# GpSimd takes the C products of the selective scan in half steps 5 to 26 of the first layer, VectorE writes their B products to PSUM, and attention 0 makes do with two PSUM banks fewer

## Chip, cores and metric

One core of a Trainium2 chip runs the whole program. The metric is the device time in microseconds of one execution. TensorE (PE) multiplies and transposes, VectorE (DVE) does elementwise work, scans and reductions, ScalarE (ACT) does activations and copies, GpSimd (POOL) does elementwise work beside them, and SyncE (SP) issues most of the DMAs.

## The reference, cut to what matters

A two-layer decoder over `x` [4, 256, 256] and a context [4, 256, 128]. Each layer adds an attention branch, a selective state space branch ("xattn") and a feed-forward branch. The change touches the attention and the state space branch of the first layer:

```python
x = x + _L0_attn_ref(_layernorm(x), ...)            # 8 heads of 32, window 64, tanh cap, softmax
x = x + _L0_xattn_ref(ctx, _layernorm(x), ...)

# inside _L0_xattn_ref, for each position of the sequence:
dA = exp(d[..., None] * A)
state = state * dA + (d * u)[..., None] * b[:, None, :]     # 256 channels x 16 states
y = einsum('bdn,bn->bd', state, c)
```

## The kernel before, in words

The 1024 tokens lie on the free axis and the 256 channels in two tiles (`DT` = 2) of 128 partitions. The state space branch is worked off in "half steps" `g`: one of the 16 states for one half (512) of the tokens, so 32 half steps a layer (`LAYER_STEPS`), 0 to 31 in the first layer. Each is one [128, 2, 512] array, 1024 elements per partition, and passes four engines:

- ACT, `ssm_da` (L509): `dA = exp(DEL * A)`, two instructions, each counted in `da_ready`.
- DVE, `ssm_dbu` (L838), the **B product**: `hS = DU * B`, both inputs in SBUF; counted in `dbu_ready`.
- DVE, `ssm_scan` (L846), the **scan**: the recurrence over `dA` and the B product, in place in `hS`; counted in `scan_done`.
- DVE, the **C product** (L849): `hS = hS * C`, in place; counted in `c_ready`.
- PE, `acc` (L1230): eight 128x128 transposes that add the result to PSUM banks 6 and 7; counted in `acc_mm`.

`hS` and `dA` are rings of four half steps, `BCb` holds B and C of four half steps (SP loads one when the C product four half steps back is done, `load_bc`). Every engine has its own instruction stream in the order of the code, and waits on counting semaphores.

Beside the first layer's half steps runs attention 0. Before half step 5, GpSimd does the rotary and norm arithmetic of q, k and v (L375 to L385) between DVE's reductions. Then there are 16 units `u` (`UNITS0`: sequence, group, pair of heads). PE does for each unit the scores `s0(u + 1)` (L1320 to L1322), the transposes back `pv0_tr(u - 1)` (L1346), the product with the values `pv0(u)` (L1334), and then the `acc` of one half step. ACT does the tanh (L575), the exponentials (L581, L582), a copy (L568) and the `ssm_da` of one half step. DVE does `at0(u)` (a reciprocal L944 and a product L947, both read PSUM) after half step `AT0_AT[u]` = 12 + u, so one unit after each of half steps 12 to 27. After unit 8 (`A_TR_UNIT`) the first half of the attention output is transposed (L1354, copied at L954 and L562). Scores used PSUM banks 0 to 3 in two pairs, `pv0` bank 4, `pv0_tr` bank 5. Half steps 28 to 31, the output projection, the gate and the feed-forward branch follow.

In the second layer (half steps 32 to 63) and in the expert stage at the end nothing is changed. The expert stage (L420, L423 on GpSimd, L1203, L1206 on DVE) and one small operation of the routing (L1178) appear in the rows below.

Of the kernel before, what the change touches and what calls it, by code (L numbers as in the profile page):

```python
# [52 lines left out]
STEPS = 2 * 2 * DS  # L53
PAIR_STEPS = DS
# [31 lines left out]
def build(nc, io, out):  # L86
    ctx = ExitStack()
    with ctx:
# [174 lines left out]
        CONV_BANK = [0, 4]  # L263
        ACC_BANK = 6
# [73 lines left out]
        def _(pool):  # L338
# [48 lines left out]
            gp.memset(V0[:, :, D0:D0 + 1], 1.0).then_inc(s["pt0_fill"], 1)  # L387
            ln_rstd(1)
# [64 lines left out]
        def _(act):  # L453
# [101 lines left out]
            for i in range(8):  # L555
                act.wait_ge(s["tr0_mm"], i + 1)
                g, part, hf = i // 4, (i // 2) % 2, i % 2
                dst = (qT0, kT0)[part][:, g, 512 * hf:512 * hf + 512]
                sc.copy(dst, ps[:, 2 + i % 4, :]).then_inc(s["tr0_copied"], 1)
            def a_tr_copy(hf):  # L560
                act.wait_ge(s["a_tr_mm"], 2 * hf + 1)
                sc.copy(aT0[:, 0, 512 * hf:512 * hf + 512], ps[:, 4, :]).then_inc(s["a_tr_act"], 1)  # L562

            def pv0_copy(u):
                act.wait_ge(s["pv0_mm"], u + 1)
                if u:
                    act.wait_ge(s["pv0_tr"], u)
                sc.copy(O0, ps[0:D0 + 1, 4, :]).then_inc(s["pv0_copied"], 1)  # L568

            for u in range(UNITS0):  # L570
# [3 lines left out]
                sb0 = 2 * (u % 2)  # L574
                sc.activation(TH0[u % 2], ps[:, sb0:sb0 + 2, 0:W0 + P], ACT.Tanh, scale=SCORE0).then_inc(s["s0_tanh"], 1)  # L575
# [195 lines left out]
        def _(dve):  # L771
# [56 lines left out]

            def ssm_dbu(g):

                l, pr, n = place(g)
                dve.wait_ge(ld_bc[g % SB_LOADS], 16 * (g // SB_LOADS + 1))
                if g % LAYER_STEPS == 0:
                    dve.wait_ge(s["du_ready"], l + 1)
                if g >= RING:
                    dve.wait_ge(s["acc_mm"], g - RING + 1)
                b = BCb[g % SB_LOADS][:, 0:1, :].broadcast_to([P, DT, HALF])
                v.tensor_tensor(ring(hS, g), DU[:, :, pair(pr)], b, ALU.mult).then_inc(s["dbu_ready"], 1)  # L838

            def ssm_scan(g):  # L840
# [96 lines left out]
            def at0(u):  # L937
# [5 lines left out]
                o = ps[:, 5, 0:4 * (D0 + 1)].rearrange("p (h d) -> p h d", d=D0 + 1)  # L943
# [268 lines left out]
        def _(pe):  # L1212
            mm, tr = nc.tensor.matmul, nc.tensor.transpose

            def conv(l, tiles=range(DT)):

                pe.wait_ge(s["lw_ready"], l + 1)
                pe.wait_ge(ld["ctx"], 16)
                for d in tiles:
# [75 lines left out]
            for i in range(8):  # L1295
# [3 lines left out]
                for t in range(4):  # L1299
# [6 lines left out]
                    last = tr(ps[:, 2 + i % 4, P * t:P * t + P], src, ident[:])  # L1306
# [3 lines left out]
            def s0(u):  # L1310
# [15 lines left out]
            def pv0(u):  # L1326
# [6 lines left out]
                for kb_ in range(2):  # L1333
                    last = mm(ps[0:D0 + 1, 4, :], V0[:, 2 * b + kb_, D0 * g:D0 * g + D0 + 1], PT0[u % 2][:, :, kb_, :],  # L1334
                              start=(kb_ == 0), stop=(kb_ == 1))
                last.then_inc(s["pv0_mm"], 1)

            def pv0_tr(u):
# [4 lines left out]
                for t in range(2):  # L1343
                    for r in range(2):
                        c = (2 * t + r) * (D0 + 1)
                        last = tr(ps[:, 5, c:c + D0 + 1], O0[:, S * r + P * t:S * r + P * t + P], ident[0:D0 + 1, 0:D0 + 1])  # L1346
                last.then_inc(s["pv0_tr"], 1)

            def a_tr(hf):

                pe.wait_ge(s["at0_ready"], UNITS0 if hf else A_TR_UNIT + 1)
                for c in range(HC):
                    for t in range(4):
                        last = tr(ps[:, 4 + c, P * t:P * t + P], H[:, 4 * hf + t, P * c:P * c + P], ident[:])  # L1354
# [486 lines left out]
```

## Time and profile before

| | |
|---|---|
| median of 3 runs | 987.07 us (983.51 to 987.46) |
| the profiled execution | 985.21 us, its span 983.4 us |
| mean granted TensorE clock | 0.912 of full |
| PE busy | 806.8 us (82%) |
| DVE busy | 741.3 us (75%) |
| ACT busy | 459.3 us (47%) |
| POOL busy | 243.4 us (25%) |
| chain that ended last | PE 46%, DVE 30%, issue 11%, ACT 8%, POOL 2% |

Busy shares are over the whole span. The half steps that change start at about 112 us and end at about 230 us of it.

### The profile page before, as it was taken

The numbers are of one execution on the slowest core, as the hardware profiler recorded it, in microseconds if no ns is written. First come the engines' busy times: TensorE is split into PE (matmuls) and PEld (weight loads), VectorE is DVE, ScalarE is ACT, GpSimd is POOL, SyncE is SP. The second block draws the span as 40 slices with busy tenths as digits, with TensorE's granted clock in tenths as the row PEclk, the third lists the DMA queues.
The fourth block names the chain that finished last, engine by engine and source line by source line (L and its number), as shares of the span: only waits on it lengthen the run. The fifth ranks groups of instructions, "written<-read, shape, count | busy, mean of one in ns | idle before, by whom it ended". The sixth has DMA issues, their size and how long they took to land.

```text
span 983.4 us, 11811 instructions
## 1 busy us (share of the span) xinstructions
PE 806.8 (82%) x3952; PEld 577.3 (59%) x3952; DVE 741.3 (75%) x1080; ACT 459.3 (47%) x951; POOL 243.4 (25%) x162
## 2 busy tenths in 40 slices
PE   6822549997788996698998987988984789999997
PEld 3312435555533473466665665656763579999996
DVE  4599899999987897789899788869956744434443
ACT  1422445563114302467666656646773434544542
POOL 1072200000223012101011021111002447666663
PEclk9765658998899999899999999999997799999999
DMA  4222133221502022011111111011200034433431
GB/s 158 91 95 84 44 107 107 107 86 65 203 2 90 22 86 86 3 46 40 63 44 44 44 44 43 23 43 43 88 1 0 1 128 156 149 139 129 157 129 43
DMA packets 24176, 74.60 MB, mean 76 GB/s; under 512 B 3088, under 2 KB 5664, under 8 KB 23744
## 3 DMA queue, kind: packets, MB, share of 16 engines
q1 hardware_dynamic: 23776, 71.51, 20.7%
q10 hardware_dynamic: 352, 2.49, 0.8%
q8 instruction: 25, 0.41, 0.2%
q14 instruction: 23, 0.19, 0.1%
HBM read 72.55 MB, written 1.44 MB: 75 GB/s over the span
## 4 chain that ended last, share of the span: by engine, by line
PE 46%; DVE 30%; issue 11%; ACT 8%; POOL 2%; DMA 0%; POOLq 0%; DVEq 0%; SPq 0%; ACTq 0%
DVE hS L846 10%; PE ps L1457 6%; PE ps L1571 6%; PE ps L1572 6%; PE ps L1573 6%; DVE hS L838 4%; PE ps L1420 4%; PE ps L1536 3%; PE ps L1437 2%; PE ps L1524 2%; PE ps L1222 2%; PE ps L1230 2%; DVE arena L1097 2%; ACT dA L509 1%; PE ps L1515 1%
## 5 line engine op out<-in xcount | busy, mean ns | idle before, releaser
L846 DVE TENSOR_TENSOR_SCAN hS<-dA,hS 128x1024 f32<-128x1024 f32 x64 | 157.8, 2465 | 21.7 <-ACT dA L509 20.5
L1230 PE MATMUL ps<-ident,hS 128*128 128x128 f32 x512 | 75.8, 299 | 49.6 <-DVE hS L849 49.4
L1203 DVE SCALAR_TENSOR_TENSOR arena<-ps,arena 128x1024 f32<-128x1024 f32 x32 | 39.2, 1225 | 102.0 <-ACT arena L724 93.1
L1230 PEld LDWEIGHTS ps<-ident,hS 128*128 128x128 f32 x512 | 64.2, 154 | 77.7 <-DVE hS L849 59.3
L1457 PE MATMUL ps<-WB,hT 128*128 128x512 f32 x192 | 88.7, 606 | 3.8 <-DVE arena L1078 2.0
L509 ACT ACTIVATE dA<-DEL,negA 128x510 f32<-128x510 f32 x128 | 84.8, 717 | 12.3 <-DVE hS L846 11.8
L423 POOL TENSOR_TENSOR MHl<-arena,MHh 128x1024 fp32r<-128x1024 f32 x34 | 81.7, 2404 | 16.7 <-ACT MHh L727 16.7
L849 DVE TENSOR_TENSOR hS<-hS,BCb 128x1024 f32<-128x1024 f32 x64 | 83.6, 1306 | 2.2
L1571 PE MATMUL ps<-Wh,MHh 128*128 128x256 f32 x272 | 77.8, 286 | 6.0 <-POOL MHl L423 6.0
L409 POOL TENSOR_SCALAR jst<-jst 128x8 f32<-128x8 f32 x20 | 12.3, 613 | 279.6 <-DVE jst L1086 279.6
L838 DVE TENSOR_TENSOR hS<-DU,BCb 128x1024 f32<-128x1024 f32 x64 | 77.8, 1216 | 0.1
L1572 PE MATMUL ps<-Wl,MHh 128*128 128x256 f32 x272 | 77.5, 285 | 0.0
L1573 PE MATMUL ps<-Wh,MHl 128*128 128x256 f32 x272 | 77.5, 285 | 0.0
L354 POOL TENSOR_SCALAR lnve<-lnmv 128x4 f32<-128x4 f32 x12 | 4.9, 405 | 268.3 <-DVE lnmv L868 268.2
L1536 PE MATMUL ps<-WA,arena 128*128 128x256 f32 x256 | 65.8, 380 | 2.5 <-DVE X L1135 2.5
L420 POOL TENSOR_TENSOR Wl<-WB,Wh 128x512 fp32r<-128x512 f32 x34 | 47.3, 1393 | 64.2 <-ACT Wh L708 64.2
L1457 PEld LDWEIGHTS ps<-WB,hT 128*128 128x128 f32 x192 | 37.1, 195 | 41.8 <-issue 40.8
L1515 PE MATMUL ps<-ident,arena 128*128 128x128 f32 x192 | 33.5, 285 | 29.4 <-ACT arena L677 24.2
L1571 PEld LDWEIGHTS ps<-Wh,MHh 128*128 128x128 f32 x272 | 52.7, 194 | 8.2 <-POOL MHl L423 7.0
L1571 PE MATMUL ps<-hTh,Wh 128*128 128x512 f32 x136 | 53.8, 396 | 0.0
L1572 PE MATMUL ps<-hTl,Wh 128*128 128x512 f32 x136 | 53.5, 394 | 0.0
L1572 PEld LDWEIGHTS ps<-Wl,MHh 128*128 128x128 f32 x272 | 52.8, 194 | 1.2
(206 smaller groups left out, 1889.5 us busy)
## 6 DMA issues: line engine op xcount, KB each, us to landing
BCb<-bc_dram SPq DMA_DIRECT2D x64, 512.0 KB, 3.6
arena<-gate_dram SPq DMA_DIRECT2D x32, 512.0 KB, 3.7
WB<-in_we SPq DMA_DIRECT2D x34, 256.0 KB, 2.7
WB<-in_wqkv SPq DMA_DIRECT2D x1, 3072.0 KB, 12.9
WA<-in_wo ACTq DMA_DIRECT2D x1, 2048.0 KB, 7.7
WA<-in_ffn SPq DMA_DIRECT2D x1, 1408.0 KB, 6.5
pkb<-in_pk SPq DMA_DIRECT2D x2, 698.0 KB
X<-in_x SPq DMA_DIRECT2D x1, 1024.0 KB, 7.4
```

Source lines behind the costliest of these rows:

```text
L420: gp.tensor_tensor(Wl[:, slot, :], src, Wh[:, slot, :].bitcast(F32), ALU.subtract).then_inc(s["w_lo"], 1)
L423: gp.tensor_tensor(MHl[:, p, :], MH[p], MHh[:, p, :].bitcast(F32), ALU.subtract).then_inc(s["m_lo"], 1)
L509: sc.activation(bands2(ring(dA, g)[:, d, :]), bands2(DEL[:, d, pair(pr)]), ACT.Exp, scale=negA[:, d * DS + n:d * DS + n + 1]).then_inc(s[" ...
L838: v.tensor_tensor(ring(hS, g), DU[:, :, pair(pr)], b, ALU.mult).then_inc(s["dbu_ready"], 1)
L846: v.tensor_tensor_scan(f(h), f(a), f(h), 0.0, ALU.mult, ALU.add).then_inc(s["scan_done"], 1)
L849: v.tensor_tensor(h, h, c, ALU.mult).then_inc(s["c_ready"], 1)
L1230: last = mm(ps[:, ACC_BANK + j // 2, 256 * (j % 2) + P * d:256 * (j % 2) + P * d + P], src[:, d, P * j:P * j + P], ident[:], start=(first ...
L1457: last = mm(ps[:, bank + t, :], hT[:, c, P * (2 * b + t):P * (2 * b + t) + P], WB[:, c, c0:c0 + 512], start=(c == 0), stop=(c == HC - 1))
L1536: last = mm(ps[:, 5, 256 * t:256 * t + 256], aT1[u % 2][:, P * t:P * t + P], WO1[:, h, :], start=(h == 0 and t == 0), stop=(h == H1 - 1), ...
L1571: mm(out, wh, xh, start=start, stop=False, **kw)
L1572: mm(out, wh, xl, start=False, stop=False, **kw)
L1573: return mm(out, wl, xh, start=False, stop=stop, **kw)
```

## The change

A constant `POOL_STEPS = range(5, 27)` names the half steps. For these, DVE writes the B product to PSUM banks 4 and 5 instead of `hS`, waiting for the scan before it, since there is one such buffer; the scan reads it from there and writes `hS`; DVE does no C product; GpSimd does it, in its stream between attention 0's preparation and the next norm. PSUM banks 4 and 5 were attention 0's, which now has one pair of banks for scores (0, 1) and banks 2 and 3 for `pv0` and `pv0_tr`, so `s0(u + 1)` waits for the tanh of unit `u` instead of `u - 1`.

```diff
+POOL_STEPS = range(5, 27)
...
+            def times_c(g):
+
+                pool.wait_ge(s["scan_done"], g + 1)
+                pool.wait_ge(ld_bc[g % SB_LOADS], 16 * (g // SB_LOADS + 1))
+                h = ring(hS, g)
+                gp.tensor_tensor(h, h, BCb[g % SB_LOADS][:, 1:2, :].broadcast_to([P, DT, HALF]), ALU.mult).then_inc(s["c_ready"], 1)
+
+            for g in POOL_STEPS:
+                times_c(g)
             ln_rstd(1)
             ln_rstd(2)
...
-                sb0 = 2 * (u % 2)
-                sc.activation(TH0[u % 2], ps[:, sb0:sb0 + 2, 0:W0 + P], ACT.Tanh, scale=SCORE0).then_inc(s["s0_tanh"], 1)
+                sc.activation(TH0[u % 2], ps[:, 0:2, 0:W0 + P], ACT.Tanh, scale=SCORE0).then_inc(s["s0_tanh"], 1)
...
+            def dbu(g):
+                return ps[:, DBU_BANK:DBU_BANK + 2, :] if g in POOL_STEPS else ring(hS, g)
+
             def ssm_dbu(g):
...
                 b = BCb[g % SB_LOADS][:, 0:1, :].broadcast_to([P, DT, HALF])
-                v.tensor_tensor(ring(hS, g), DU[:, :, pair(pr)], b, ALU.mult).then_inc(s["dbu_ready"], 1)
+                if g in POOL_STEPS:
+                    dve.wait_ge(s["scan_done"], g)
+                    dve.wait_ge(s["qkv0_copied"], NT)
+                v.tensor_tensor(dbu(g), DU[:, :, pair(pr)], b, ALU.mult).then_inc(s["dbu_ready"], 1)
...
-                v.tensor_tensor_scan(f(h), f(a), f(h), 0.0, ALU.mult, ALU.add).then_inc(s["scan_done"], 1)
+                v.tensor_tensor_scan(f(h), f(a), f(dbu(g)), 0.0, ALU.mult, ALU.add).then_inc(s["scan_done"], 1)
+                if g in POOL_STEPS:
+                    return
                 dve.wait_ge(s["scan_done"], g + 1)
+                if g == POOL_STEPS.stop:
+                    dve.wait_ge(s["c_ready"], g)
...
+                if l:
+                    pe.wait_ge(s["scan_done"], POOL_STEPS.stop)
...
-                if u >= 2:
-                    pe.wait_ge(s["s0_tanh"], u - 1)
+                if u:
+                    pe.wait_ge(s["s0_tanh"], u)
                 q0 = S * b
                 for i in range(2):
-                    r, k = 2 * rp + i, 2 * (u % 2) + i
+                    r, k = 2 * rp + i, i
...
-                    last = mm(ps[0:D0 + 1, 4, :], V0[:, 2 * b + kb_, D0 * g:D0 * g + D0 + 1], PT0[u % 2][:, :, kb_, :],
+                    last = mm(ps[0:D0 + 1, 2, :], V0[:, 2 * b + kb_, D0 * g:D0 * g + D0 + 1], PT0[u % 2][:, :, kb_, :],
```

The other lines of the diff only change bank numbers (`tr0` copies, `O0`, `at0`, `a_tr`).

DVE's stream in half steps 13 and 14, each followed by the `at0` of a unit, before (the names in square brackets are the semaphores that an instruction and the wait instructions ahead of it wait for, in their order):

```order
L838 TENSOR_TENSOR hS<-DU,BCb 128x1024 [waits acc_mm,ld_bc1]
L846 SCALAR_TENSOR_TENSOR hS<-dA,hS 128x1024 [waits da_ready,dbu_ready]
L849 TENSOR_TENSOR hS<-hS,BCb 128x1024 [waits scan_done]
L944 RECIPROCAL rden<-ps 128x4 [waits at0_ready,pv0_tr]
L947 TENSOR_TENSOR H<-ps,rden 128x2x64 [waits at0_den]
L838 TENSOR_TENSOR hS<-DU,BCb 128x1024 [waits acc_mm,ld_bc2]
L846 SCALAR_TENSOR_TENSOR hS<-dA,hS 128x1024 [waits da_ready,dbu_ready]
L849 TENSOR_TENSOR hS<-hS,BCb 128x1024 [waits scan_done]
```

and the same place in the changed kernel, where L854 is the B product, L862 the scan, and L964 and L967 are `at0`:

```order
L854 TENSOR_TENSOR ps<-DU,BCb 128x1024 [waits scan_done,qkv0_copied,acc_mm,ld_bc1]
L862 SCALAR_TENSOR_TENSOR hS<-dA,ps 128x1024 [waits da_ready,dbu_ready]
L964 RECIPROCAL rden<-ps 128x4 [waits at0_ready,pv0_tr]
L967 TENSOR_TENSOR H<-ps,rden 128x2x64 [waits at0_den]
L854 TENSOR_TENSOR ps<-DU,BCb 128x1024 [waits scan_done,qkv0_copied,acc_mm,ld_bc2]
L862 SCALAR_TENSOR_TENSOR hS<-dA,ps 128x1024 [waits da_ready,dbu_ready]
```

The C product is gone from DVE's stream, and the B product's list of waits is two longer, with `scan_done` at its head.

GpSimd's stream from the last step of attention 0's preparation on, in the changed kernel; in the kernel before, the first two rows were followed directly by the norm's (L354 there):

```order
L387 TENSOR_TENSOR arena<-arena 128x3072 [waits rope0_rs]
L389 MEMSET arena 128x8 [waits rope0_done]
L395 TENSOR_TENSOR hS<-hS,BCb 128x1024 [waits ld_bc1,scan_done]
L395 TENSOR_TENSOR hS<-hS,BCb 128x1024 [waits ld_bc2,scan_done]
L395 TENSOR_TENSOR hS<-hS,BCb 128x1024 [waits ld_bc3,scan_done]
L395 TENSOR_TENSOR hS<-hS,BCb 128x1024 [waits ld_bc0,scan_done]
```

There are 22 such rows, one for each of half steps 5 to 26, each with `scan_done` as its last wait.

## Rows read from the trace of the kernel before

**Rows 1.** The page: the chain's shares by line, and the costliest groups.
```profile
DVE hS L846 10%; PE ps L1457 6%; PE ps L1571 6%; PE ps L1572 6%; PE ps L1573 6%; DVE hS L838 4%; PE ps L1420 4%; PE ps L1536 3%; PE ps L1437 2%; PE ps L1524 2%; PE ps L1222 2%; PE ps L1230 2%; DVE arena L1097 2%; ACT dA L509 1%; PE ps L1515 1%
...
L423 POOL TENSOR_TENSOR MHl<-arena,MHh 128x1024 fp32r<-128x1024 f32 x34 | 81.7, 2404 | 16.7 <-ACT MHh L727 16.7
...
L420 POOL TENSOR_TENSOR Wl<-WB,Wh 128x512 fp32r<-128x512 f32 x34 | 47.3, 1393 | 64.2 <-ACT Wh L708 64.2
```

**Rows 2.** Table by stretches: us; busy of PE, PEld, DVE, ACT, POOL; clock; DMA.
```profile
127.00:154.00 27.00, 16.59 (x56) 11.13 (x57) 26.59 (x20) 9.94 (x18) 0.00 (x0) 0.51 0.29 101
155.00:195.00 40.00, 39.11 (x210) 23.63 (x210) 38.43 (x39) 23.13 (x42) 0.00 (x0) 1.00 0.28 97
480.00:560.00 80.00, 71.45 (x377) 52.52 (x378) 75.61 (x132) 52.59 (x149) 10.06 (x10) 1.00 0.13 41
```

**Rows 3.** Timeline of DVE (start, us, line), half steps 11 and 12.
```profile
144.44 2.29 DVE L846 TENSOR_TENSOR_SCAN hS<-dA,hS 128x1024 f32<-128x1024 f32 x1
146.76 1.22 DVE L849 TENSOR_TENSOR hS<-hS,BCb 128x1024 f32<-128x1024 f32 x1
...
149.16 2.29 DVE L846 TENSOR_TENSOR_SCAN hS<-dA,hS 128x1024 f32<-128x1024 f32 x1
```

**Rows 4.** Timeline of DVE, half steps 26 and 27.
```profile
224.96 2.29 DVE L846 TENSOR_TENSOR_SCAN hS<-dA,hS 128x1024 f32<-128x1024 f32 x1
...
228.43 0.17 DVE L944 RECIPROCAL rden<-ps 128x4 f32<-128x4 f32 x1
...
228.85 1.22 DVE L838 TENSOR_TENSOR hS<-DU,BCb 128x1024 f32<-128x1024 f32 x1
230.10 2.29 DVE L846 TENSOR_TENSOR_SCAN hS<-dA,hS 128x1024 f32<-128x1024 f32 x1
```

**Rows 5.** Timeline of PE, half steps 17 and 18: first scores of two units.
```profile
180.83 0.30 PE L1320 MATMUL ps<-mask,identb 128*128 128x320 bf16 x1
...
185.91 0.30 PE L1320 MATMUL ps<-mask,identb 128*128 128x320 bf16 x1
```

**Rows 6.** Waits of DVE, 103 to 290 us: total, times, longest.
```profile
DVE hS L846 <- ACT dA L509: 2.5, 1, 2.5
DVE rden L944 <- PE ps L1346: 1.9, 1, 1.9
...
DVE hT L954 <- PE ps L1354: 1.2, 1, 1.2
```

**Rows 7.** Timeline of DVE and POOL, attention 0's preparation at 102 us.
```profile
102.41 0.26 DVE L932 SCALAR_TENSOR_TENSOR arena<-arena 128x96 f32<-128x96 f32 x1
102.58 1.22 DVE L838 TENSOR_TENSOR hS<-DU,BCb 128x1024 f32<-128x1024 f32 x1
102.75 6.28 POOL L385 TENSOR_TENSOR arena<-arena 128x3072 f32<-128x3072 f32 x1 [15.71 <-DVE arena L932]
103.84 7.33 DVE L846 TENSOR_TENSOR_SCAN hS<-dA,hS 128x1024 f32<-128x1024 f32 x1
```

**Rows 8.** Timeline of DVE and POOL, the preparation at 64 us.
```profile
63.94 7.43 POOL L381 TENSOR_TENSOR arena<-arena 128x2560 f32<-128x2560 f32 x1
66.04 6.41 DVE L849 TENSOR_TENSOR hS<-hS,BCb 128x1024 f32<-128x1024 f32 x1
```

**Rows 9.** Timeline of DVE and POOL, the routing at 781 us.
```profile
780.64 2.35 POOL L423 TENSOR_TENSOR MHl<-arena,MHh 128x1024 fp32r<-128x1024 f32 x1 [5.12 <-ACT MHh L727]
780.70 2.35 DVE L1178 TENSOR_SCALAR arena<-arena 128x96 f32<-128x96 f32 x1
```

**Rows 10.** Timeline of DVE and POOL, one expert at 821 us.
```profile
821.55 2.40 POOL L423 TENSOR_TENSOR MHl<-arena,MHh 128x1024 fp32r<-128x1024 f32 x1
...
823.33 1.22 DVE L1203 SCALAR_TENSOR_TENSOR arena<-ps,arena 128x1024 f32<-128x1024 f32 x1 [3.04 <-ACT arena L724]
```

**Rows 11.** Timeline of ACT, then of DVE, at half step 6.
```profile
119.42 1.31 ACT L509 ACTIVATE dA<-DEL,negA 128x510 f32<-128x510 f32 x2
...
120.83 2.29 DVE L846 TENSOR_TENSOR_SCAN hS<-dA,hS 128x1024 f32<-128x1024 f32 x1 [2.54 <-ACT dA L509]
```

More of the change, by code:

```diff
@@ L263, in build @@
         CONV_BANK = [0, 4]
+        DBU_BANK = 4
         ACC_BANK = 6
@@ L558, in _ @@
                 dst = (qT0, kT0)[part][:, g, 512 * hf:512 * hf + 512]
-                sc.copy(dst, ps[:, 2 + i % 4, :]).then_inc(s["tr0_copied"], 1)
+                sc.copy(dst, ps[:, i % 4, :]).then_inc(s["tr0_copied"], 1)
             def a_tr_copy(hf):
                 act.wait_ge(s["a_tr_mm"], 2 * hf + 1)
-                sc.copy(aT0[:, 0, 512 * hf:512 * hf + 512], ps[:, 4, :]).then_inc(s["a_tr_act"], 1)
+                sc.copy(aT0[:, 0, 512 * hf:512 * hf + 512], ps[:, 2, :]).then_inc(s["a_tr_act"], 1)
             def pv0_copy(u):
@@ L567, in pv0_copy @@
                     act.wait_ge(s["pv0_tr"], u)
-                sc.copy(O0, ps[0:D0 + 1, 4, :]).then_inc(s["pv0_copied"], 1)
+                sc.copy(O0, ps[0:D0 + 1, 2, :]).then_inc(s["pv0_copied"], 1)
             for u in range(UNITS0):
@@ L942, in at0 @@
                     dve.wait_ge(s["at0_ready"], u)
-                o = ps[:, 5, 0:4 * (D0 + 1)].rearrange("p (h d) -> p h d", d=D0 + 1)
+                o = ps[:, 3, 0:4 * (D0 + 1)].rearrange("p (h d) -> p h d", d=D0 + 1)
                 v.reciprocal(rden0[:], o[:, :, D0 * (1 - g)]).then_inc(s["at0_den"], 1)
@@ L953, in a_tr_copy @@
                 dve.wait_ge(s["a_tr_mm"], 2 * hf + 2)
-                v.tensor_copy(aT0[:, 1, 512 * hf:512 * hf + 512], ps[:, 5, :]).then_inc(s["a_tr_dve"], 1)
+                v.tensor_copy(aT0[:, 1, 512 * hf:512 * hf + 512], ps[:, 3, :]).then_inc(s["a_tr_dve"], 1)
             for g in range(4, LAYER_STEPS - 4):
@@ L1305, in _ @@
                         src = K40[:, 4 * hf + t, g, :]
-                    last = tr(ps[:, 2 + i % 4, P * t:P * t + P], src, ident[:])
+                    last = tr(ps[:, i % 4, P * t:P * t + P], src, ident[:])
                 last.then_inc(s["tr0_mm"], 1)
@@ L1345, in pv0_tr @@
                         c = (2 * t + r) * (D0 + 1)
-                        last = tr(ps[:, 5, c:c + D0 + 1], O0[:, S * r + P * t:S * r + P * t + P], ident[0:D0 + 1, 0:D0 + 1])
+                        last = tr(ps[:, 3, c:c + D0 + 1], O0[:, S * r + P * t:S * r + P * t + P], ident[0:D0 + 1, 0:D0 + 1])
                 last.then_inc(s["pv0_tr"], 1)
@@ L1353, in a_tr @@
                     for t in range(4):
-                        last = tr(ps[:, 4 + c, P * t:P * t + P], H[:, 4 * hf + t, P * c:P * c + P], ident[:])
+                        last = tr(ps[:, 2 + c, P * t:P * t + P], H[:, 4 * hf + t, P * c:P * c + P], ident[:])
                     last.then_inc(s["a_tr_mm"], 1)
```

## Prediction

> **What bounds the kernel now.** I read the page first, for which lines hold the chain that ended last; then the table by stretches, for which engine is full where the change works; then DVE's timeline through one half step of each kind; then what DVE waited for; and last the places where GpSimd and DVE work at the same time, because the change makes them do so 22 times.
>
> DVE's scan is the line with the largest share of the chain (10%), its B product has 4% [rows 1]. Between 127 and 154 us DVE is busy for 26.59 of 27 us and PE for 16.59, at a granted clock of 0.51, its lower level of 1.2 GHz. Between 155 and 195 us, with attention units beside the half steps, both are full: DVE 38.43 and PE 39.11 of 40 us, PE now at 2.4 GHz [rows 2]. A half step without a unit takes DVE 4.72 us from scan to scan (144.44 to 149.16): scan 2.29, C product 1.22, B product 1.22, with small overlaps [rows 3]. With a unit it takes 5.14 us (224.96 to 230.10); from the unit's reciprocal to the next B product are 0.42 us [rows 4]. PE's period there is 5.08 us (180.83 to 185.91) [rows 5]. So DVE sets the pace up to half step 12, and after it DVE and PE set it together. DVE's idle time in this part is small: 2.5 us before the scan of half step 6, for ACT, and 1.9 and 1.2 us around the transposes after unit 8, for PE [rows 6].
>
> The stretch that I compare runs from the scan of half step 6 at 120.83 us [rows 11] to that of half step 27 at 230.10 us [rows 4]: **109.27 us for 21 half steps**.
>
> **The change part by part.** *Removed from DVE:* 22 C products of 1.22 us. If nothing took their place, a half step would go from 4.72 to about 3.6 us, and from 5.14 to about 4.0.
>
> *Added on GpSimd:* 22 products of 128x1024. The nearest row is the same operation on as many elements in the expert stage, 2.404 us over 34 of them [rows 1]. In themselves they would fit beside a scan of 2.29 us plus a B product.
>
> *Whether the two run side by side* is what decides. The trace says when they do not. At 103.84 us a scan with both inputs in SBUF starts 1.09 us into a GpSimd product and takes 7.33 us in place of 2.29; it ends at 111.17, 2.14 us after GpSimd's end at 109.03 [rows 7]. At 66.04 us a C product takes 6.41 us and ends at 72.45, 1.08 us after GpSimd's end at 71.37 [rows 8]. So a DVE instruction with two SBUF inputs stands until GpSimd's ends. The order is by who starts first: the B product at 102.58 us, 0.17 us ahead of GpSimd, keeps its 1.22 us [rows 7]; a small DVE operation at 780.70 us, 0.06 us behind GpSimd's start, is held for GpSimd's whole 2.35 us [rows 9]. A lead of 0.06 us is enough.
>
> The scan is taken out of this: it now has one SBUF input and one in PSUM, and such an instruction of the expert stage keeps 1.22 us while GpSimd works beside it (823.33 against an end at 823.95) [rows 10]. That row also says that reading PSUM costs nothing over SBUF. But the B product still reads DU and B from SBUF, and the C product and the next B product are both released by the same `scan_done`.
>
> *Who starts first after a scan.* GpSimd: its instruction waits on `scan_done` itself, and in rows 7 it starts 0.08 us after the DVE instruction that it waits for (102.67 to 102.75). DVE: in half steps 12 to 26 it does the unit's two operations first, 0.42 us. In half steps 6 to 11 the B product comes directly, but with four semaphores, `scan_done` at the head of the list and two others between it and the instruction. What a wait ahead of an instruction takes is seen at half step 6: ACT's end at 120.73, scan at 120.83, 0.10 us with one such wait [rows 11]; with more behind it I take about 0.2 us. So **GpSimd starts first every time**, and DVE's next B product stands until the C product ends.
>
> *The half step then is* 0.08 (GpSimd's start after the scan) + 2.40 (C product) + 1.08 (what remains of the B product after GpSimd's end, rows 8) + 0.03 (B product to scan, 103.80 to 103.84 in rows 7) + 2.29 (scan) = **5.88 us**, with a unit or without, since the unit's 0.42 us lie beside the C product. The scan and the C product never overlap, so writing the B product to PSUM gains nothing.
>
> *The sum.* 21 x 5.88 = 123.5 us, less 109.27, is **+14.2 us**. The first C product (half step 5) costs nothing: it and the B product behind it end at about 119.4 us, and the scan of half step 6 waits for ACT until 120.83 in any case. The 3.1 us of idle time around unit 8 are inside the 109.27; in the changed kernel DVE waits for PE while the C product runs anyway. After half step 27 DVE's stream is as before and has little idle time, so the delay reaches the end.
>
> *The price of the C product.* The trace does not show this very operation. Lower bound: the 2560-element product of rows 8, which itself stood until the scan before it ended (about 66.01), then took 5.36 us, 2.09 ns per element, 2.14 us for 1024. Upper bound: twice the 512-element product, 2 x 1.39 = 2.79 us [rows 1]. I take 2.40, the same shape. The ends give 5.62 and 6.27 us per half step, +8.7 and +22.4 us. The Trainium skill (GPSIMD Engine Reference, section 3.1, Elementwise) has 4497 ns for an elementwise operation of two inputs over 2048 elements; halved, as an estimate, that is 2.25 us, and the sum would be +11.1 us.
>
> *Small parts, together.* DVE writing to PSUM is in no row; reading is free by rows 10, I bound it by 0.05 us per half step to either side, 1 us in all, and take nothing. The single pair of score banks: in steady state a tanh follows its scores at once and PE comes to the next scores only after a `pv0` and an `acc`, so the wait is over by then; only at the first unit does PE stand for about 0.8 us, with half steps of work in hand. The ring of four: a C product ends about 2.5 us after its scan instead of 1.2, while `acc_mm` and the B and C loads are asked for three half steps later. PE's new `scan_done` wait in `conv` is met before PE comes to it.
>
> **The rivals.**
> *A, DVE is first in half steps 6 to 11* (its waits cost less than GpSimd's 0.08 us). Then a B product of 1.22, a C product beside the scan, and 3.57 us per half step: 6 x 3.57 + 15 x 5.88 = 109.6, +0.3 us, 987.4. Rows 3 speak for it (0.03 us from a scan to the instruction that waits on it alone); the list of waits speaks against it.
> *B, faster: the two run side by side throughout* (a product into PSUM is not held, or DVE gets its B product in first even behind the unit). DVE needs 3.57 and 4.0 us, and PE becomes the bound at 5.08 us per unit: 6 x 1.15 + 15 x 0.06 = 7.8 us saved, 979.3. It decides if the C products end after the following B product has run at its plain 1.22 us. Rows 7 to 9 speak against it. By the Trainium skill (SBUF — State Buffer, section "Who interferes with whom") two SBUF inputs on DVE stand against a GpSimd operation that reads SBUF, whichever starts first holding the shared ports throughout; by that rule rival B needs DVE to start first behind the units too, and the trace agrees with the rule in rows 7 to 10.
> *C, slower still: PE falls back to the lower clock.* It would be busy for 5.08 of 5.88 us, 86%. Where five units of fifteen fall to 1.2 GHz, each needs PE for about 10.2 us in place of 5.88; two of the five are taken up by half steps that PE is ahead, and three cost 4.3 us each, 13 us, 1014. Against it: 71.45 of 80 us busy (89%) kept the clock at 1.00 [rows 2].
>
> **How the numbers follow.** The forecast has 0.74, A 0.10, B 0.10, C 0.06. The profiled execution took 985.21 us; the same +14.2 on the median of 987.07 gives **1001.3 us**. The range reaches down to A's end at 987 and up to 1009 (the upper bound of the C product, 22.4 us, is the end itself). About 0.5%, 5 us, is what a measurement of this kernel can tell from no change. Faster: B, 0.10. Same: A, 0.10. Slower: the forecast and C, 0.80.
>
> **What would show it.** Right: GpSimd's C products start about 0.08 us after each scan; B products in half steps 6 to 27 show some 3 us in place of 1.22 (about 3.3 without a unit before them, 3.1 with one); scans stay at 2.29; scans are 5.88 us apart. Wrong: B products at 1.22 us and C products of 3.5 us or more (DVE first: rival A or B), scans above 2.3 us (PSUM as a scan input is dear, or it is held too), or C products well off 2.40.

## The result, and the profile of the changed kernel

| | before | changed |
|---|---|---|
| median of 4 runs of each, us | 985.29 (982.5 to 987.46) | 1003.56 (1002.07 to 1005.95) |
| ratio of the times, 95% interval | | 1.0194 (1.0157 to 1.0232) |
| profiled execution, us (its span) | 985.21 (983.4) | 1002.07 (1000.3) |
| scan of half step 6 to scan of half step 27, us | 109.27 | 124.84 |

The change makes the kernel 1.9% slower. In the profiled executions the span is 16.9 us longer, and the stretch in which the C products moved is 15.6 us longer. The forecast was 1001.3 us and +14.2 us.

The page of the changed kernel, with the span, the busy times and the shares of the chain that ended last (it answers to [rows 1]):

```profile
span 1000.3 us, 11858 instructions
PE 808.5 (81%) x3952; PEld 578.7 (58%) x3952; DVE 753.5 (75%) x1058; ACT 459.3 (46%) x951; POOL 293.7 (29%) x184
DVE hS L862 7%; PE ps L1479 6%; PE ps L1593 6%; DVE ps L854 5%; PE ps L1594 5%; PE ps L1595 5%; PE ps L1442 4%; PE ps L1558 3%; PE ps L1459 2%; DVE hS L854 2%; PE ps L1252 2%; PE ps L1546 2%; PE ps L1244 2%; DVE arena L1117 2%; ACT dA L520 2%
```

L862 is the scan now and L854 the B product. The B product that writes to PSUM ("ps") stands in the chain with 5% of its own, beside 2% for the half steps that still write it to SBUF ("hS"). The scan's share fell from 10% to 7%. A hold by GpSimd shows as nothing but a larger share of the B product; L395 isn't among the lines of the chain, since no semaphore marks the end of the hold.

The same instructions by line, all half steps (duration in ns, least, median and longest; then first and last start, and the shape; L395 is GpSimd's C product):

```profile
L854 DVE TENSOR_TENSOR hS<-DU,BCb x42: 1191/1218/3198, 51.7 to 732.9; 128x1024 f32<-128x1024 f32 x42
L854 DVE TENSOR_TENSOR ps<-DU,BCb x22: 1224/3208/3317, 110.6 to 234.7; 128x1024 f32<-128x1024 f32 x22
L862 DVE TENSOR_TENSOR_SCAN hS<-dA,ps x22: 2286/2287/2287, 111.9 to 237.9; 128x1024 f32<-128x1024 f32 x22
L395 POOL TENSOR_TENSOR hS<-hS,BCb x22: 2341/2352/2368, 114.3 to 240.3; 128x1024 f32<-128x1024 f32 x22
```

These four rows are nearly the whole story. The same B product has a median of 1.22 us in the half steps where GpSimd does no C product and 3.21 us where it does. Of the 22 B products that come behind a C product of GpSimd's, 18 take 3.19 to 3.32 us. The other four, of half steps 21 to 24, come later because DVE waited for PE at unit 8: two run after GpSimd's end at 1.22 us, two catch its last part and take 1.99 and 2.75 us. The scan stays at 2.29 us in all 22 half steps. GpSimd's product is even, 2.34 to 2.37 us, so it is never the one that is held.

DVE and GpSimd through one half step without a unit (11 to 12) and one with a unit (18 to 19); start, duration, line, and in brackets the idle time before with what ended it:

```profile
148.10 2.29 DVE L862 TENSOR_TENSOR_SCAN hS<-dA,ps 128x1024 f32<-128x1024 f32 x1
150.47 2.34 POOL L395 TENSOR_TENSOR hS<-hS,BCb 128x1024 f32<-128x1024 f32 x1 [3.49 <-DVE hS L862]
150.59 3.31 DVE L854 TENSOR_TENSOR ps<-DU,BCb 128x1024 f32<-128x1024 f32 x1 [0.20 <-DVE hS L862]
153.93 2.29 DVE L862 TENSOR_TENSOR_SCAN hS<-dA,ps 128x1024 f32<-128x1024 f32 x1
...
188.99 2.29 DVE L862 TENSOR_TENSOR_SCAN hS<-dA,ps 128x1024 f32<-128x1024 f32 x1
191.19 0.16 DVE L964 RECIPROCAL rden<-ps 128x4 f32<-128x4 f32 x1
191.35 2.36 POOL L395 TENSOR_TENSOR hS<-hS,BCb 128x1024 f32<-128x1024 f32 x1 [3.49 <-DVE hS L862]
191.38 0.29 DVE L967 TENSOR_TENSOR H<-ps,rden 128x128 f32<-128x128 f32 x1
191.59 3.21 DVE L854 TENSOR_TENSOR ps<-DU,BCb 128x1024 f32<-128x1024 f32 x1
194.83 2.29 DVE L862 TENSOR_TENSOR_SCAN hS<-dA,ps 128x1024 f32<-128x1024 f32 x1
```

The scan ends at 150.39. GpSimd starts 0.08 us later, DVE 0.20 us later, and the B product then ends at 153.90, 1.09 us after GpSimd's end at 152.81. From scan to scan that is 5.83 us without a unit and 5.84 with one, where [rows 3] and [rows 4] had 4.72 and 5.14. GpSimd's idle time of 3.49 us before each product shows that it had time to spare: it is not the bound, only in the way.

What DVE waited for between 103 and 300 us (total, times, longest; [rows 6] before):

```profile
DVE rden L964 <- PE ps L1368: 4.7, 3, 3.3
DVE hT L974 <- PE ps L1376: 2.1, 1, 2.1
...
DVE ps L854 <- DVE hS L862: 1.4, 7, 0.2
DVE hS L862 <- ACT dA L520: 1.2, 1, 1.2
```

The third row shown is the 0.20 us by which DVE comes late, seven times (half steps 5 to 11). Rows one and two are waits for PE around the transposes after unit 8. A held B product isn't in this view at all: the hold is booked as duration.

The changed kernel by stretches (busy time of PE, PEld, DVE, ACT, POOL, then the granted clock of PE, DMA share, GB/s), the first two to set beside [rows 2]:

```profile
127.00:154.00 27.00, 12.00 (x48) 8.93 (x49) 25.82 (x11) 8.74 (x15) 11.74 (x5) 0.57 0.23 79
160.00:198.00 38.00, 36.89 (x195) 21.77 (x194) 37.55 (x28) 23.09 (x41) 14.91 (x7) 1.00 0.29 96
199.00:209.00 10.00, 4.77 (x12) 2.11 (x12) 7.83 (x7) 3.24 (x6) 2.89 (x2) 0.50 0.34 107
428.00:448.00 20.00, 16.94 (x85) 12.99 (x84) 16.06 (x28) 13.69 (x40) 2.10 (x3) 0.91 0.07 27
608.00:638.00 30.00, 25.87 (x119) 17.61 (x118) 25.91 (x48) 16.56 (x50) 2.74 (x2) 0.94 0.11 36
```

DVE still reads as full (37.55 of 38 us), but some 2 us of each half step are an instruction that stands. PE holds 2.4 GHz beside the units and is at 1.2 GHz around unit 8 (0.50). What PE did before that, in the changed kernel and then in the kernel before (the first transposes after unit 8):

```profile
203.40 1.97 PE L1376 MATMUL ps<-ident,H 128*128 128x128 f32 x8 [5.33 <-DVE H L967]
```

```profile
194.27 1.09 PE L1354 MATMUL ps<-ident,H 128*128 128x128 f32 x8 [0.89 <-DVE H L947]
```

The transposes need DVE's result of unit 8. DVE now takes 5.84 us for a half step of which PE's part takes 5.08. PE, behind at first (15.00 busy of 15 us from 160 to 175 and again from 175 to 190), waits for DVE for the first time at 191 us, and at unit 8 it stands for 5.33 us in place of 0.89. The granted clock is 0.50 from 199 to 203 us, where PE does nothing, and the same eight transposes then take 1.97 us in place of 1.09.

**Where the 16.9 us are.** The scan of half step 6 starts at 118.91 us, 1.9 us earlier than before. Of this 1.7 us are there already at the scan of half step 4 (102.11 us against 103.84), where nothing is changed yet; over the thirteen traces of this case that scan starts between 100.6 and 104.1 us. The stretch adds 15.6. From the scan of half step 27 to the end 3.2 us more pass (756.6 against 753.3 us). Two steps of about 1.2 and 1.7 us make most of the last term; they lie in the second layer's attention, between 428 and 448 and between 608 and 638 us, where the granted clock was 0.91 and 0.94 in this execution and 1.00 in the execution before, over the same work. They don't belong to the change: the changed kernel with earlier units (the last experiment below) takes 751.5 us from the same scan to the end, and two executions of one other kernel, B product first with units earlier, take 760.2 and 755.1 us.

### The profile page after: what moved, and what is told of

The parts are those of the page before. It is cut to its first block, busy times and chain, and to the rows that moved or that the text cites. A ratio compares the mean times of both kernels' runs of the same rounds, so it can differ in the third digit from the quotient of the medians.

```text
span 1000.3 us, 11858 instructions
## 1 busy us (share of the span) xinstructions
PE 808.5 (81%) x3952; PEld 578.7 (58%) x3952; DVE 753.5 (75%) x1058; ACT 459.3 (46%) x951; POOL 293.7 (29%) x184
## 4 chain that ended last, share of the span: by engine, by line
PE 47%; DVE 29%; issue 11%; ACT 8%; POOL 2%; DMA 1%; DVEq 0%; POOLq 0%; SPq 0%; ACTq 0%
DVE hS L862 7%; PE ps L1479 6%; PE ps L1593 6%; DVE ps L854 5%; PE ps L1594 5%; PE ps L1595 5%; PE ps L1442 4%; PE ps L1558 3%; PE ps L1459 2%; DVE hS L854 2%; PE ps L1252 2%; PE ps L1546 2%; PE ps L1244 2%; DVE arena L1117 2%; ACT dA L520 2%
## 5 line engine op out<-in xcount | busy, mean ns | idle before, releaser
L862 DVE TENSOR_TENSOR_SCAN hS<-dA,hS 128x1024 f32<-128x1024 f32 x42 | 105.9, 2522 | 18.4 <-ACT dA L520 17.9
L434 POOL TENSOR_TENSOR MHl<-arena,MHh 128x1024 fp32r<-128x1024 f32 x34 | 81.8, 2405 | 16.9 <-ACT MHh L737 16.9
L395 POOL TENSOR_TENSOR hS<-hS,BCb 128x1024 f32<-128x1024 f32 x22 | 51.8, 2352 | 83.4 <-DVE hS L862 83.4
L854 DVE TENSOR_TENSOR ps<-DU,BCb 128x1024 f32<-128x1024 f32 x22 | 63.7, 2894 | 1.4 <-DVE hS L862 1.4
L869 DVE TENSOR_TENSOR hS<-hS,BCb 128x1024 f32<-128x1024 f32 x42 | 56.6, 1348 | 1.4
L854 DVE TENSOR_TENSOR hS<-DU,BCb 128x1024 f32<-128x1024 f32 x42 | 54.1, 1289 | 0.1
```

Source lines behind the costliest of these rows:

```text
L395: gp.tensor_tensor(h, h, BCb[g % SB_LOADS][:, 1:2, :].broadcast_to([P, DT, HALF]), ALU.mult).then_inc(s["c_ready"], 1)
L434: gp.tensor_tensor(MHl[:, p, :], MH[p], MHh[:, p, :].bitcast(F32), ALU.subtract).then_inc(s["m_lo"], 1)
L854: v.tensor_tensor(dbu(g), DU[:, :, pair(pr)], b, ALU.mult).then_inc(s["dbu_ready"], 1)
L862: v.tensor_tensor_scan(f(h), f(a), f(dbu(g)), 0.0, ALU.mult, ALU.add).then_inc(s["scan_done"], 1)
L869: v.tensor_tensor(h, h, c, ALU.mult).then_inc(s["c_ready"], 1)
```

## The experiments

The forecast rests on three claims: (1) a two-SBUF-input instruction of DVE stands while GpSimd's runs, and all of the loss is that; (2) who starts first after a scan decides, by hundredths of a microsecond; (3) the new waits, the PSUM destination and the single pair of score banks cost nothing. The eleven runs, of ten kernels, take these apart. All compute the whole reference. Line numbers shift by one or two where an edit adds lines. Each ratio is against the kernel before, run on the same chip.

### First four: who is first, and what the rest costs

**B product first.** In GpSimd's `times_c`, one wait more:

```
             def times_c(g):
+                pool.wait_ge(s["dbu_ready"], g + 2)
                 pool.wait_ge(s["scan_done"], g + 1)
```

GpSimd's C product of half step g now waits until DVE's B product of half step g + 1 has ended.

> GpSimd's C product g waits, beside the scan g, for the B product g + 1; all else as in the changed kernel. Theory (the one that starts first holds the other off, and in the changed kernel GpSimd is first): every B product is back at 1.22 us, the C product starts 0.1 us after it and runs 2.35 us beside the scan, which has one input in PSUM and stays at 2.29. Half steps 6 to 11 take 3.6 to 3.75 us in place of 5.84, those with a unit are set by PE at 5.08 us: some 14 us less than the changed kernel from there alone and 11 us from the rest, a time of about 978 to 980 us, 5 to 8 us under the kernel before. Rival (two engines' operations on SBUF hold each other off whatever the inputs are): the scan is held until the C product ends, half steps of 1.2 + 2.4 + 2.2 = 5.8 us, about 1003 us as the changed kernel.

Measured: 981.85 us against 984.42, ratio 0.9982 (0.9947 to 1.0016); the stretch takes 106.55 us. DVE and GpSimd over two half steps:

```profile
123.39 1.23 DVE L855 TENSOR_TENSOR ps<-DU,BCb 128x1024 f32<-128x1024 f32 x1 [0.20 <-DVE hS L863]
124.66 2.29 DVE L863 TENSOR_TENSOR_SCAN hS<-dA,ps 128x1024 f32<-128x1024 f32 x1
124.70 2.36 POOL L396 TENSOR_TENSOR hS<-hS,BCb 128x1024 f32<-128x1024 f32 x1 [4.82 <-DVE ps L855]
127.15 1.23 DVE L855 TENSOR_TENSOR ps<-DU,BCb 128x1024 f32<-128x1024 f32 x1 [0.20 <-DVE hS L863]
128.42 2.29 DVE L863 TENSOR_TENSOR_SCAN hS<-dA,ps 128x1024 f32<-128x1024 f32 x1
```

Scan (2.29) and C product (2.36) run side by side at their own prices, the B product is back at 1.23, and a half step without a unit takes 3.76 us. A single line of waiting turns 1.9% slower into no measurable difference. But it is less than was expected (978 to 980 us). DVE's waits of this kernel from 103 to 300 us, one of the instructions behind the first of them, the last C product on GpSimd with what stands around it, and three stretches of the table:

```profile
DVE rden L965 <- PE ps L1369: 22.2, 14, 4.1
...
DVE hS L870 <- POOL hS L396: 2.3, 1, 2.3
```

```profile
148.06 0.18 DVE L965 RECIPROCAL rden<-ps 128x4 f32<-128x4 f32 x1 [2.33 <-PE ps L1369]
...
227.46 2.29 DVE L863 TENSOR_TENSOR_SCAN hS<-dA,hS 128x1024 f32<-128x1024 f32 x1
227.50 4.40 POOL L396 TENSOR_TENSOR hS<-hS,BCb 128x1024 f32<-128x1024 f32 x1 [1.50 <-DVE hS L855]
...
232.01 1.23 DVE L870 TENSOR_TENSOR hS<-hS,BCb 128x1024 f32<-128x1024 f32 x1 [2.26 <-POOL hS L396]
```

```profile
122.00:143.00 21.00, 12.12 (x56) 8.49 (x55) 19.61 (x12) 10.90 (x19) 11.72 (x5) 0.66 0.30 108
143.00:160.00 17.00, 17.00 (x73) 9.91 (x72) 10.68 (x11) 7.26 (x13) 7.05 (x3) 0.76 0.26 93
160.00:190.00 30.00, 30.00 (x157) 17.49 (x155) 23.19 (x23) 19.16 (x35) 14.02 (x6) 1.00 0.31 106
```

Half steps 6 to 11 save six times 0.96 us, 5.8 us. When the units begin, PE is busy for 17.00 of 17 us at a clock of 0.76, and DVE waits 2.33 and 2.67 us for it: the next two half steps take 6.30 and 6.64 us. After that PE sets a pace of 5.08 us and DVE has nothing to give. Of the 5.8 us 2.7 are left at the scan of half step 27, and most of these go in the very next step. The scan of half step 27 has two SBUF inputs again ("dA,hS"), starts 0.04 us ahead of GpSimd's last C product and holds it (4.40 us), and DVE's C product of half step 27 waits 2.26 us for that one. From scan 27 to scan 28 pass 8.69 us in place of 6.47. So the handing back of the C products costs 2.2 us once, in every kernel here in which the B product goes first over all 22 half steps.

**The wait on the B product itself.** The changed kernel, with the wait for the scan moved to the head of the four in the source. In the program that is built the first of them stands in the instruction itself and the others in wait instructions ahead of it (in the lists of the two streams `ld_bc`, the first in the source, is named last), so that now the B product carries the wait for the scan:

```
+                if g in POOL_STEPS:
+                    dve.wait_ge(s["scan_done"], g)
                 dve.wait_ge(ld_bc[...], ...)
...
                 if g in POOL_STEPS:
-                    dve.wait_ge(s["scan_done"], g)
                     dve.wait_ge(s["qkv0_copied"], NT)
```

> The changed kernel, but the B product waits for scan_done in the instruction itself and its other waits lie ahead of it, so DVE can start 0.03 us after the scan, ahead of GpSimd's 0.08. This is the forecast's rival A made on purpose. Theory (a lead of 0.05 us is enough): half steps 6 to 11 fall from 5.84 to 3.6 us, 13 us less; those with a unit, where DVE does the two small operations first, stay at 5.84; in all about 990 us. Rival (the order of start is not what decides; GpSimd has priority, or the lead is too small): no change, 1003 us.

Measured: 991.46 us against 984.42, ratio 1.0079 (1.0046 to 1.0113); the stretch takes 115.69 us. First the one half step of the six in which DVE was late for another reason, then a regular one:

```profile
124.14 2.38 POOL L395 TENSOR_TENSOR hS<-hS,BCb 128x1024 f32<-128x1024 f32 x1 [0.20 <-DVE hS L863]
125.32 2.28 DVE L855 TENSOR_TENSOR ps<-DU,BCb 128x1024 f32<-128x1024 f32 x1 [1.27 <-PE ps L1253]
...
133.55 1.23 DVE L855 TENSOR_TENSOR ps<-DU,BCb 128x1024 f32<-128x1024 f32 x1
133.59 3.38 POOL L395 TENSOR_TENSOR hS<-hS,BCb 128x1024 f32<-128x1024 f32 x1 [0.21 <-DVE hS L863]
134.81 2.29 DVE L863 TENSOR_TENSOR_SCAN hS<-dA,ps 128x1024 f32<-128x1024 f32 x1
137.13 1.23 DVE L855 TENSOR_TENSOR ps<-DU,BCb 128x1024 f32<-128x1024 f32 x1
```

At 133.55 the B product is 0.04 us ahead of GpSimd and keeps 1.23 us; GpSimd's product shows 3.38 in place of 2.35. At 125.32 the B product comes 1.18 us behind and is held. So this is rival A made on purpose: 3.59 us in five of the six half steps without a unit, 5.84 in most of those with a unit (two at its start and two around unit 8 wait for PE and take 6.24 to 8.25), because there the unit's operations make DVE late again. The order of the waits in the source is worth 2.25 us in each half step where DVE is not late for another reason.

**The C product back on DVE.** GpSimd's loop and the early return are taken out; B products to PSUM, the new waits and the two banks fewer stay:

```
-            for g in POOL_STEPS:
-                times_c(g)
...
-                if g in POOL_STEPS:
-                    return
...
-                if g == POOL_STEPS.stop:
-                    dve.wait_ge(s["c_ready"], g)
```

> The C products are back on DVE; the B products still go to PSUM banks 4 and 5 with their extra waits, and attention 0 keeps its two banks fewer. Theory (all of the loss is GpSimd's C product in front of the B product): half steps of 4.72 and 5.14 us, scans of 2.29, 985 to 988 us as the kernel before. Rival (PSUM as output or input, the extra waits or the single pair of score banks cost part of it): half steps 0.1 to 0.7 us longer, up to 1003 us.

Measured: 986.9 us against 984.42, ratio 1.0016 (0.9982 to 1.005). Half steps take 4.72 and 5.14 us, the B product 1.23, the scan 2.29, as before; the stretch, 111.07 us, is 1.8 us longer, nearly all of it in one longer stall at unit 8 (8.57 us for a half step that took 7.18). The kernel before with nothing but earlier units, which has all its score banks, shows 7.89 and 7.75 us there, so a stall of this size doesn't need the change. Claim (3) holds to within the interval: these parts together cost at most 5 us, the B product, the scan and the regular half steps show no cost, and whether the single pair of score banks has a part in the stall isn't shown.

**The B product in SBUF again**, GpSimd as in the change:

```
-                return ps[:, DBU_BANK:DBU_BANK + 2, :] if g in POOL_STEPS else ring(hS, g)
+                return ring(hS, g)
```

> The changed kernel with the B product written to hS in SBUF, so the scan has two SBUF inputs again; the waits and GpSimd's C product stay. Theory (GpSimd starts first, so a scan never runs beside a C product, and the way through PSUM gains nothing): scans stay at 2.29 us, half steps at 5.84, 1003 us. Rival (the way through PSUM takes a collision out that is there otherwise): scans or C products longer, half steps above 6 us, over 1006 us.

Measured: 1004.34 us against 984.42, ratio 1.0181 (1.0129 to 1.0234), the changed kernel's own time. Half steps away from unit 8 take 5.82 to 5.85 us, the stretch 125.77 us. While GpSimd is first, scan and C product never overlap, and the PSUM route gains nothing.

### Four more: what PSUM is for, and what PE gives back

**B product first, but in SBUF** (the edits of the first and the fourth together).

> As e1_b_first, but the B product goes to hS in SBUF, so the scan has two SBUF inputs while GpSimd's C product is due beside it. Theory (two SBUF inputs on DVE and a GpSimd operation that reads SBUF hold each other off; a scan with one input in PSUM does not): the scan starts 0.01 us ahead of the C product and holds it off, or the other way round; either way the three run one after another, half steps without a unit 5.6 to 5.9 us in place of 3.76, those with one about as long, 998 to 1004 us. Rival (the way through PSUM makes no difference, only the order does): as e1_b_first, 982 us.

Measured: 1003.11 us against 987.17, ratio 1.0177 (1.0136 to 1.0219). DVE and GpSimd over one half step:

```profile
124.48 2.29 DVE L863 TENSOR_TENSOR_SCAN hS<-dA,hS 128x1024 f32<-128x1024 f32 x1
124.52 4.39 POOL L396 TENSOR_TENSOR hS<-hS,BCb 128x1024 f32<-128x1024 f32 x1 [4.69 <-DVE hS L855]
126.97 3.03 DVE L855 TENSOR_TENSOR hS<-DU,BCb 128x1024 f32<-128x1024 f32 x1 [0.20 <-DVE hS L863]
130.03 2.29 DVE L863 TENSOR_TENSOR_SCAN hS<-dA,hS 128x1024 f32<-128x1024 f32 x1
```

The scan now has two SBUF inputs ("dA,hS") and is 0.04 us ahead, so GpSimd stands until 126.77, ends at 128.91 after 2.14 us of its own, and holds the next B product. The half step is 5.55 us and the stretch 120.51 us. Beside the first experiment (3.76 us, "dA,ps") this is what the PSUM destination is worth once DVE is first: 1.8 us a half step. The Trainium skill (SBUF — State Buffer, section "Who interferes with whom") says that DVE instructions with at most one SBUF input, outside DVE's 2-port modes, don't contend with GpSimd, that those with two contend with a GpSimd instruction that reads SBUF, and that the order of issue decides who blocks. These runs agree: the scan with one SBUF input and the C product take 2.29 and 2.36 us side by side, and with two SBUF inputs GpSimd stands where DVE is first (4.39 us here) and DVE where GpSimd is (3.31 us in the changed kernel).

**B product first in half steps 5 to 11 alone** (`POOL_STEPS = range(5, 12)` with the wait of the first experiment).

> As e1_b_first, but only half steps 5 to 11 (those without an attention unit) use GpSimd; 12 to 26 are as in the kernel before. Theory (from half step 12 on PE sets the pace in e1_b_first, so DVE's saving there is worth nothing): half steps 6 to 11 at 3.76 us, those with a unit at 5.14 in place of 5.08, a time within 2 us of e1_b_first, 981 to 984 us. Rival (the C products behind the units are worth something too, DVE's idle time before at0 being PE's lower clock only by chance): 3 us or more above e1_b_first.

Measured: 986.75 us against 987.17, ratio 1.0003 (0.9971 to 1.0034), stretch 107.92 us. Half steps 6 to 10 take 3.75 or 3.76 us and half step 11 takes 3.50, then come 7.34 and 5.61, then 5.14. The head start is the same, but most of the first loss has another cause. GpSimd and DVE at half step 12:

```profile
143.25 4.38 POOL L396 TENSOR_TENSOR hS<-hS,BCb 128x1024 f32<-128x1024 f32 x1 [1.16 <-DVE hS L855]
...
147.74 1.23 DVE L870 TENSOR_TENSOR hS<-hS,BCb 128x1024 f32<-128x1024 f32 x1 [2.24 <-POOL hS L396]
```

The scan of half step 12 has two SBUF inputs and holds the last C product, for which DVE then waits 2.24 us: the handing back of the first experiment, now inside the stretch. For PE DVE waits only 0.39 us in half step 13, so this run doesn't show by itself that PE takes the head start. The absolute time expected (981 to 984) was missed. The stretch is 1.4 us longer than with all 22, but it holds the 2.2 us that lie behind the stretch there, and the intervals overlap: whether the later 15 bring anything stays open.

**B product first, waits direct, units earlier.** If PE's late start gives the gain away, giving PE its units sooner must keep it. The edit of the first experiment, the moved wait of the second, and:

```
-AT0_AT = [12 + u for u in range(UNITS0)]
+AT0_AT = [8 + 5 * u // 4 for u in range(UNITS0)]
```

> As e1_b_first, with scan_done waited for in the B product itself (0.03 us in place of 0.20 after the scan), and attention 0's units begun at half step 8 and spread at five half steps for four units (AT0_AT = 8 + 5u // 4), so PE begins its share earlier. Theory (what is left in e1_b_first is PE, which stands idle before half step 12 and is full after it): the stretch from scan 6 to scan 27 falls from 106.6 to about 94 us, 968 to 974 us, under both kernels. Rival (PE's lower clock in its first units, or ACT, takes the gain): 979 us or more.

Measured: 977.17 us against 987.17, ratio 0.9893 (0.9845 to 0.9942). Its table for the stretch from 125 to 190 us, and its waits from 103 to 300 us:

```profile
125.00:190.00 65.00, 61.06 (x327) 36.55 (x326) 52.42 (x51) 39.89 (x72) 32.11 (x14) 1.00 0.35 114
```

```profile
DVE rden L966 <- PE ps L1370: 15.7, 13, 3.3
...
DVE hS L871 <- POOL hS L396: 2.2, 1, 2.2
```

The stretch takes 99.06 us, 10.2 less than before. PE holds 2.4 GHz over these 65 us (1.00; the profile of its repeat below has 0.94) and is busy for 61.06 of 65 us, where the kernel before has this over the same 65 us:

```profile
125.00:190.00 65.00, 53.12 (x245) 32.35 (x243) 63.84 (x56) 33.69 (x60) 0.00 (x0) 0.79 0.31 107
```

Expected were 94 us for the stretch and 968 to 974 in all, so the direction was right and the size too large: by some 5 us in the stretch, where 15.7 us of waits for PE remain, at PE's pace of 5.08 us and around unit 8, and by 2.2 us behind it, where the C products are handed back (8.28 us from scan 27 to scan 28, against 6.06 in the control below).

**The kernel before with the same earlier units**, as the control.

> The kernel before, with nothing but the units begun at half step 8 and spread at five half steps for four units. Theory (before, DVE is full in all half steps, and spreading PE's work moves only the 3 us in which DVE waits for PE): the stretch from scan 6 to scan 27 stays at 105 to 109 us, 981 to 985 us. Rival (the spread alone brings what e8_b_first_units_early brings): 975 us or less.

Measured: 984.43 us against 987.17, ratio 0.9984 (0.9954 to 1.0014), stretch 111.13 us (105 to 109 expected, missed by a longer stall at unit 8). Nothing measurable: DVE is full there, and earlier units only put their 0.42 us into other half steps.

### The last three

**The version with earlier units once more**, since its first interval came from four runs.

> The kernel of e8_b_first_units_early once more, in more rounds, beside the two runs that take its parts away. Theory: 0.985 to 0.993 of the kernel before. Rival (the 1.1% of e8 was a lucky set of runs): 0.995 or more.

Measured: 977.75 us against 986.81, ratio 0.992 (0.9891 to 0.9948), over 11 runs; stretch 99.93 us. Both intervals lie below 1. It is faster than the kernel before by about 0.8 to 1.1%, and than the changed kernel by some 2.6% (977.75 against 1003.56, of different batches).

**B product first with the direct wait, units as they were.**

> e8_b_first_units_early with attention 0's units back at half steps 12 to 27, that is e1_b_first with scan_done waited for in the B product itself. Theory (the early units bring nearly all of e8's gain, since with the units late PE sets the pace): half steps 7 to 11 at 3.59 us in place of 3.76, a gain of under 1 us that PE swallows at half step 12; a ratio to the kernel before of 0.995 to 1.0. Rival (the shorter wait is what brings it): 0.990 or less.

Measured: 986.42 us against 986.81, ratio 0.9992 (0.9956 to 1.0027), stretch 105.93 us. 3.59 us per half step without a unit (3.90 in one), then 6.47 and 7.79 us waiting for PE. The earlier units alone and the B product first alone bring nothing measurable; both together do. Earlier units with the first experiment's wait, without the direct one, were not run, so what the direct wait adds to the faster version isn't shown.

**The changed kernel with earlier units** (the edit of `AT0_AT` alone).

> The changed kernel, GpSimd still first, with attention 0's units begun at half step 8 as in e8. Theory (with GpSimd first a half step is 5.84 us whatever PE does): the stretch from scan 6 to scan 27 at 122.6 to 125 us, 1000 to 1004 us. Rival (the early units alone mend the change): 990 us or less.

Measured: 999.84 us against 986.81, ratio 1.0141 (1.0102 to 1.0179), stretch 124.91 us. One half step:

```profile
126.67 2.35 POOL L395 TENSOR_TENSOR hS<-hS,BCb 128x1024 f32<-128x1024 f32 x1 [3.49 <-DVE hS L862]
126.80 3.31 DVE L854 TENSOR_TENSOR ps<-DU,BCb 128x1024 f32<-128x1024 f32 x1 [0.20 <-DVE hS L862]
```

5.84 us as in the changed kernel, wherever the units stand (only the two half steps around unit 8 are longer, 6.62 and 7.31 us). The loss in each regular half step has nothing to do with PE.

## Why the prediction was right, and where its sizes were off

**GpSimd starts first every time: right.** 22 of 22 C products start 0.08 us after their scan. 18 of the 22 B products behind them start 0.20 us after it, or 0.32 behind a unit; four come 0.77 to 3.68 us after it, held up by PE at unit 8. The undoing of this one step (the B product first) takes the whole loss away, 1.0194 to 0.9982, with everything else of the change in place. Moving a wait by a few lines (0.04 us of lead) takes it away in just those half steps in which DVE then is first. Where the B product is written makes no difference to the hold (1.0181 with SBUF); its two SBUF inputs and the order do.

**The half step of 5.88 us: right to 0.04.** Measured 5.84. Only the C product differs, 2.35 where 2.40 was taken from the expert stage's row. The held B products took 3.31 and 3.21 us, said were about 3.3 and 3.1. The remainder after GpSimd's end (1.09 for 1.08), the 0.03 us to the scan and the scan's 2.29 stood. The C product had 2.35 us of its own when free and 2.14 when it came out of a hold, the "lower bound" from such a row: both rows were right, for two different cases.

**"The 3.1 us of idle time around unit 8 are inside the 109.27; in the changed kernel DVE waits for PE while the C product runs anyway": this step failed.** The C product covers only a part. Before, the two half steps around unit 8 took 7.01 and 7.18 us, 3.9 more than two regular ones; now 6.62 and 7.23, 2.2 more, where the sum had nothing. In the other three kernels with GpSimd first over the units they are 2.2 to 3.2 more. PE has stood for 5.33 us in place of 0.89 before the transposes and is at its lower clock there (0.50 from 199 to 209 us). DVE waits 2.1 us in place of 1.2 for the transposes, and 3.3 in place of 1.9 for the next unit, to which it comes sooner without a C product of its own; both waits reach past the C product's end. The full sum is 21 x 5.84 = 122.6, and 2.2, less 109.3: +15.5, measured +15.6, against +14.2 predicted. The same omission is in rival A's 109.6 us; the kernel that makes A happen took 115.69, with 6.24, 6.47, 6.61 and 8.25 us for half steps that wait for PE, and one of six that DVE lost.

**"The delay reaches the end": right, plus 3.2 us** that the sum did not have, from a lower granted clock in two stretches of the second layer. The executions of the kernel before in later batches lie between 979 and 991 us with mean clocks of 0.908 to 0.92, so a shift of this size is within what the same kernel does, and the changed kernel with earlier units doesn't have it (751.5 us in place of 756.6). The start of half step 6 came 1.9 us earlier, which offset part of it. So the time came out nearer than the change did: 1001.3 forecast and 1003.56 measured, but +14.2 against +16.9 in the profiled executions and +18.3 between the medians. The forecast stood on a median of 987.07 us, the result on one of 985.29; that part of the closeness is luck.

**The small parts at nothing: not contradicted**, by the kernel with C on DVE (1.0016, 0.9982 to 1.005), except that the single pair of score banks isn't cleared at unit 8.

**The rivals.** A and B did not occur, and both can be made to. B's size was wrong: "6 x 1.15 + 15 x 0.06 = 7.8 us saved" forgets that PE does not start the units sooner because DVE arrives sooner, and has no term for the last C product. Measured was 0.2%, with a stretch 2.7 us shorter, because DVE then stood 22.2 us for PE, and with the next step 2.2 us longer, because the scan of half step 27 holds that C product. With the units placed earlier the stretch is 9 to 10 us shorter. C did not occur: PE kept 1.00 beside the units, at 36.89 busy us of 38; its clock fell at unit 8, after 5.33 us in which PE stood. The 86% that C reckons with did not come about there, since PE was still working off what it was behind. With the units earlier and GpSimd first the clock was 0.58 between 153 and 165 us, and the half steps kept 5.83 and 5.85 us, so a spell at the lower clock did not cost what C says it would.

**Left open.** The longer half steps around unit 8 were not tried by themselves (for instance with the transposes elsewhere), and they vary: in the two executions of the faster version half steps 18 and 19 take 6.50 and 5.77 us, and 6.88 and 8.23. A PSUM destination for the B product of half step 27 too, which would keep its scan from holding the last C product, was not tried. A second PSUM buffer for the B product was not tried.

## What to carry to other kernels

In these runs moving work from VectorE to an idle GpSimd could pay only where VectorE's instructions beside it didn't have two inputs in SBUF: list for every pair that will overlap which inputs lie in SBUF and who starts first. If one event releases both engines, the order is set by how the waits are written, and a wait for the other engine's neighbouring instruction can fix it for one line. Look at the last instruction of the moved row as well: here it met a scan with two SBUF inputs and cost 2.2 us, nearly all that was left of the gain. A time that is won ahead of another engine's work is only kept if that work is moved up as well; here either edit alone was worth nothing measurable, and both together about 1%.

## What the runs showed of the hardware that was not expected

- A lead of 0.04 us decides which of two instructions runs (133.55 against 133.59, and 124.48 against 124.52), and the loser stands until the winner's end.
- A held GpSimd instruction is recorded from the moment it would have started: 3.38 and 4.39 us for a product that takes 2.35. Its duration alone would have been read as a slow operation; it comes 0.04 us behind a DVE instruction each time.
- The same four waits in another order moved the start of a DVE instruction from 0.20 to 0.03 or 0.04 us after the event that it waits for.
- DVE's small product with one PSUM and one SBUF input is not held by GpSimd (0.29 us at 191.38, 0.03 us behind GpSimd's start), just as the scan with such inputs isn't (2.29 us), and a product written to PSUM takes 1.23 us, against 1.22 to SBUF.
- PE stood for 5.33 us before the transposes of unit 8; the granted clock was 0.50 while it did nothing (199 to 203 us), and eight transposes then took 1.97 us in place of 1.09.
- Placing attention units from half step 8 on raised PE's granted clock between 125 and 190 us: 1.00 and 0.94 in the two profiles of the faster version and 0.91 in the kernel before with that edit alone, against 0.79 in the kernel before. A higher clock by itself shortened nothing where DVE was full.
